# Four-layer graph network on one core: late units in another slot order, residuals moved, wide products a row earlier, last chunk in halves

## The reference

```
x = ln(x + adj @ (scale * (adj @ (x @ W0))) + bias0)
x = ln(x + relu(inv_deg * (a*adj + (1-a)*I) @ x @ W1.T + b1))
d = 1 / sqrt(rowsum(adj))
z = leaky_relu(d * (adj @ (d * x)) @ Wz + bz)
S = exp(-sqrt(dist2(z, z)) / 2), the 4 nearest of each row kept
A2 = S + adj;  d2 = 1 / sqrt(rowsum(A2))
x = ln(x + d2 * (A2 @ (d2 * x)) @ W2 + b2)
x = ln(x + relu(concat(x, adj @ x) @ W3.T + b3))
```

## Time and profile before

| | us |
|---|---|
| median of 3 runs (lowest, highest) | 1446.29 (1445.66, 1446.74) |
| the profiled execution | 1442.02 |
| its span, first to last instruction | 1440.5 |
| TensorE busy | 1389.3 (96%) |
| VectorE busy | 835.8 (58%) |
| ScalarE busy | 445.5 (31%) |
| mean granted clock of TensorE | 0.992 |

### The profile page before, as it was taken

The page is one execution under the profiler, slowest core; times in us unless marked ns, Lnnn a source line. Parts: engine busy times, 40 slices in busy tenths (PEclk is TensorE's granted clock), DMA queues, the critical chain, the costliest instruction groups (busy, mean ns, idle before and its releaser), DMA issues.

```text
span 1440.5 us, 20058 instructions
## 1 busy us (share of the span) xinstructions
PE 1389.3 (96%) x7268; PEld 731.8 (51%) x7268; DVE 835.8 (58%) x1311; ACT 445.5 (31%) x955; POOL 243.7 (17%) x354
## 2 busy tenths in 40 slices
PE   6999999999999999999999999999999979999997
PEld 4776666666544445454544444333333334444454
DVE  5878766666323533433322269999999556655044
ACT  4767665655200000000000047655555200000011
POOL 2111110110100100000000001111111177774000
PEclk9999999999999999999999999999999989999999
DMA  9999998887999969988777614014444889999862
GB/s 301 402 397 389 357 329 310 318 309 258 351 379 360 372 265 395 408 314 336 295 299 299 247 55 136 16 31 133 134 136 136 308 336 371 387 392 397 349 244 65
DMA packets 124850, 407.51 MB, mean 283 GB/s; under 512 B 10624, under 2 KB 40928, under 8 KB 103264
## 3 DMA queue, kind: packets, MB, share of 16 engines
q1 hardware_dynamic: 84704, 315.38, 59.0%
q0 software_dynamic: 20000, 74.97, 13.7%
q10 hardware_dynamic: 20064, 16.04, 3.3%
HBM read 339.77 MB, written 66.58 MB: 282 GB/s over the span
## 4 chain that ended last, share of the span: by engine, by line
PE 66%; DVE 21%; DMA 8%; ACT 2%; POOL 1%; issue 1%; ACTq 0%; DVEq 0%; SPq 0%; POOLq 0%
PE acc L1168 9%; PE acc L1170 9%; PE acc L1169 9%; DVE hT L1053 8%; PE pt L1232 6%; DVE wT L1054 5%; PE pt L1168 4%; PE pt L1170 4%; PE pt L1169 4%; DMA region<-in_adj 4%; DVE wz_sb L1054 3%; PE acc L1213 3%; PE acc L1217 3%; PE acc L1215 3%; PE pxT L1204 1%; PE pxT L1205 1%
## 5 line engine op out<-in xcount | busy, mean ns | idle before, releaser
L1232 PE MATMUL pt<-ident,region 128*128 128x128 f32 x1024 | 243.2, 277 | 19.7 <-DMA region<-in_adj 10.8
L1168 PE MATMUL acc<-region,yop 128*128 128x512 f16 x581 | 220.4, 379 | 5.1 <-DMA region<-at_scratch 5.1
L1169 PE MATMUL acc<-region,yop 128*128 128x512 f16 x581 | 220.2, 379 | 0.0
L1170 PE MATMUL acc<-region,yop 128*128 128x512 f16 x581 | 220.2, 379 | 0.0
L999 DVE SCALAR_TENSOR_TENSOR region<-pt,region 128x512 f16<-128x512 f32 x200 | 135.4, 687 | 75.2 <-ACT region L649 74.9
L1232 PEld LDWEIGHTS pt<-ident,region 128*128 128x128 f32 x1024 | 146.1, 143 | 61.9 <-issue 15.6
L695 ACT ACTIVATE region<-pt 128x512 f32<-128x512 f32 x256 | 132.8, 603 | 114.2 <-PE pt L1328 46.3
L649 ACT ACTIVATE region<-pt 128x512 f16<-128x512 f32 x200 | 117.8, 595 | 106.3 <-PE pt L1232 89.6
L1053 DVE MAX8 hT<-region 128x8 f32<-128x4096 f32 x32 | 141.3, 4414 | 2.9 <-ACT region L695 2.9
L616 ACT ACTIVATE std<-mv,eps_ln 128x4 f32<-128x4 f32 x32 | 9.5, 297 | 343.6 <-DVE mv L833 343.6
L1321 PE MATMUL pt<-yop 128*128 128x512 f16 x256 | 97.4, 380 | 8.1 <-ACT region L695 7.2
(11 more groups left out here) (235 smaller groups left out, 2219.6 us busy)
## 6 DMA issues: line engine op xcount, KB each, us to landing
region<-at_scratch SPq DMA_DIRECT2D x162, 1280.0 KB, 7.7
region<-in_adj SPq DMA_DIRECT2D x64, 1024.0 KB, 9.3
at_scratch<-region POOLq DMA_DIRECT2D x40, 768.0 KB, 7.0
at_scratch<-region POOLq DMA_DIRECT2D x40, 512.0 KB, 7.5
region<-at_scratch SPq DMA_DIRECT2D x76, 256.0 KB, 2.7
region<-at_scratch ACTq DMA_DIRECT2D x4, 1280.0 KB, 8.3
x_scratch<-xout ACTq DMA_DIRECT2D x16, 256.0 KB, 10.8
gath_all<-x_scratch POOLq DMA_DIRECT2D x12, 256.0 KB, 6.6
```

Of the source, the lines that this page charges most:

```text
L1168: nc.tensor.matmul(into, y[:, 0, kt, :], high, start=(kt == first_tile), stop=False)
L1169: nc.tensor.matmul(into, y[:, 0, kt, :], low, start=False, stop=False)
L1170: return nc.tensor.matmul(into, y[:, 1, kt, :], high, start=False, stop=(kt == last_tile))
L1232: ins = nc.tensor.transpose(pt[kt % 4][:, t * P:(t + 1) * P], nat[u % 4][:, t, (kt % TPC) * P:(kt % TPC + 1) * P], ident[:, :])
```

## The change

- Late units: the first four take slots 4, 3, 2, 1, then the order 4, 3, 0, 2, 1 repeats. ScalarE issues three of them instead of four; SyncE issues the fourth after the `y` stores and waits for the wide chunks' end only ahead of the first unit in slot 0.
- Residual rows: the four loads of x2 rows go from SyncE to ScalarE's queue. On VectorE the bias is added before the first mix, and the residuals of chunks 0 to 3 stand together ahead of the second mix tile.
- `WIDE_LAG` is 6 instead of 7; `SUMS_AHEAD` is 5 instead of 4.
- Last pass: ScalarE's copies of the next chunk stand ahead of `act_finish`; chunk 7 is made in two halves of 256 columns, in two banks, each projected, normalized and stored by itself; `finish_chunk` places are closer together.

The core of the diff:

```diff
-LATE_ORDER = [4, 3, 2, 1, 0]
+LATE_FIRST = [4, 3, 2, 1]
+LATE_ORDER = [4, 3, 0, 2, 1]
-WIDE_LAG = 7
+WIDE_LAG = 6
 WIDE_AT = {i: i - WIDE_LAG for i in range(WIDE_LAG, 32)}
-SUMS_AHEAD = 4
+SUMS_AHEAD = 5
-FINISH_AT = {(6, 0): 0, (6, 9): 1, (6, 18): 2, (6, 27): 3, (7, 4): 4, (7, 13): 5, (7, 22): 6}
-RESIDUAL_AT = {(0, 2): [0], (0, 3): [1], (0, 4): [2], (1, 1): [3], **{(c, 3): [c + 3] for c in range(1, 5)}}
+FINISH_AT = {(6, 0): 0, (6, 8): 1, (6, 16): 2, (6, 24): 3}
+FINISH_HALVES_AT = {(0, 0): 4, (0, 16): 5, (1, 0): 6}
+FIRST_HALF_AT = 18
+RESIDUAL_AT = {(0, 1): [0, 1, 2, 3], **{(c, 3): [c + 3] for c in range(1, 5)}}
...
# SyncE
-                if kt == RES_AT:
-                    sp.wait_ge(near_full, KT * NCH)
-                    for t in range(TPC):
-                        sp.dma_start(res_rows(t // 2, 0, NCH)[:, :, t % 2, :], x2_rows[:, t, :, :]).then_inc(res_loaded, 16)
...
-            sp.wait_ge(acc_full, nth(ALL, 4, WIDE - 1))
+            for b in range(2):
+                sp.wait_ge(y_stored[b], 16 * NCH // 2)
             for k in range(ACT_LATE, len(LATE)):
+                if k == LATE_TILES:
+                    sp.wait_ge(acc_full, nth(ALL, 4, WIDE - 1))
                 load_late(sp, k)
...
# ScalarE
                 if i == KT:
+                    act.wait_ge(near_full, KT * NCH)
+                    for t in range(TPC):
+                        act.dma_start(res_rows(t // 2, 0, NCH)[:, :, t % 2, :], x2_rows[:, t, :, :]).then_inc(res_loaded, 16)
                     act.wait_ge(near_used, KT - 1)
                     load_late(act, 0)
...
-            for c in range(NCH):
-                act_epilogue(act, 5, c, None)
+            turned_x3(0)
+            sums5(0)
+            for c in range(NCH - 2):
+                turned_x3(c + 1)
+                sums5(c + 1)
+                act_finish(act, 5, c)
+            turned_x3(NCH - 1)
+            sums_half(0)
+            act_finish(act, 5, NCH - 2)
+            sums_half(1)
...
# VectorE
-                    if (c, t) == (0, 1):
+                    if (c, t) == (0, 0):
                         residual_bias()
...
+            for h in range(2):
+                last_half(h)
...
# TensorE
-            wide_products(25)
+            wide_products(26)
             kept_narrow(NARROW_KEPT[1])
-            wide_products(26)
             wide_products(27)
...
+            for h in range(2):
+                pe.wait_ge(hT_ready, bank_left(NCH - 1) + h)
+                for kt in range(KT):
+                    last = half_columns(h, kt)
+                    if (h, kt) in FINISH_HALVES_AT:
+                        finish_chunk(FINISH_HALVES_AT[h, kt])
+                    if (h, kt) == (1, FIRST_HALF_AT):
+                        project_half(0)
+                last.then_inc(acc_full, 1)
+            project_half(1)
```

More of the change, by code:

```diff
@@ L62 @@
 NARROW_KEPT = [4, 5]
-ACT_LATE = 4
-RES_AT = 26
+ACT_LATE = 3
 A_SCALE = 64.0
@@ L221, in pass_acc, with half_acc @@
             return pt[AHEAD2.index(c)] if p == 2 and c in AHEAD2 else acc[par]
+        def half_acc(h):
+            return wide[1 + h][:, h * HALF:(h + 1) * HALF]
         def late_acc(p, c):
@@ L306, in gnn_kernel @@
                 + [(5, c, u) for c in range(WIDE5, NCH) for u in range(UPC)])
-        LATE_SLOTS = [LATE_ORDER[k % UPC] for k in range(len(LATE))]
+        LATE_SLOTS = LATE_FIRST + [LATE_ORDER[k % UPC] for k in range(len(LATE) - len(LATE_FIRST))]
+        LATE_TILES = LATE_SLOTS.index(0)
         def ends_chunk(k):
@@ L747, in projection_step @@
                     turned_x2(k)
+            x2_rows = x_dram[2].rearrange("(c t p) f -> p t c f", p=P, t=TPC)
             projection_step(0)
@@ L772, in _ @@
                     degrees(g)
-            act.wait_ge(yop_ready, nth(YOP, "y", NCH - 1))
-            for b in range(2):
-                act.wait_ge(y_stored[b], 16 * NCH // 2)
-            load_late(act, ACT_LATE - 1)
             act.wait_ge(xT_ready, nth(XTS, 4, NCH - 1))
@@ L1081, in _ @@
                 close_mix(c)
-            for c in range(NCH):
+            for c in range(NCH - 1):
                 epilogue(5, c, None)
+            for h in range(2):
+                last_half(h)
         def pe_turn(pe, p, c, x3=None, par=None, m=None):
@@ L1482, in finish_chunk, with project_half, half_columns @@
                     pe_turn(pe, 5, c + 1, ((c + 1) % X3_BUFFERS, (c + 1) // X3_BUFFERS + 1))
-            for c in range(WIDE5, NCH):
+            def project_half(h):
+                n = nth(ALL, 5, NCH - 1) + h
+                pe.wait_ge(hT_ready, n)
+                pe.wait_ge(xT_ready, nth(XTS, 5, NCH - 1))
+                pe.wait_ge(nat_read, n - 1)
+                for t in range(TPC)[h * TPC // 2:(h + 1) * TPC // 2]:
+                    nc.tensor.matmul(late_nat[:, t, :], xT[:, t * P:(t + 1) * P], wT[:, 1, :], start=True, stop=False)
+                    last = nc.tensor.matmul(late_nat[:, t, :], hT[:, t * P:(t + 1) * P], wT[:, 2, :], start=False, stop=True)
+                last.then_inc(nat_full, 1)
+            def half_columns(h, kt):
+                c = NCH - 1
+                if kt < KEPT:
+                    hi, lo = (kept[:, c, kt, part, h * HALF:(h + 1) * HALF] for part in range(2))
+                else:
+                    u, within = divmod(kt - KEPT, UNIT)
+                    k = LATE.index((5, c, u))
+                    slot = LATE_SLOTS[k]
+                    if within == 0:
+                        pe.wait_ge(late_loaded_unit[slot], 16 * late_loads(k))
+                    hi, lo = (ring[slot][:, within, part, h * HALF:(h + 1) * HALF] for part in range(2))
+                return products(5, half_acc(h), kt, hi, lo)
+            for c in range(WIDE5, NCH - 1):
                 for kt in range(KT):
@@ L1491, in _ @@
                 last.then_inc(acc_full, 1)
-            pe_project(pe, 5, NCH - 1)
+            for h in range(2):
+                pe.wait_ge(hT_ready, bank_left(NCH - 1) + h)
[7 more added lines that the diff above has]
+            project_half(1)
 LATE_PARAMS = 3
```

48 lines of the change are left out of this document (46 added, 2 removed).

## The result

The changed kernel takes 1470.88 us (median of 4, 1468.16 to 1474.10); beside it the kernel before took 1445.97 (median of 4, 1440.01 to 1446.74). The ratio is 1.0185, 95% interval 1.0162 to 1.0207: slower, clear of the noise; whether by 2% the interval leaves open. 1472.5 was predicted, in a range of 1453 to 1483. The profiled execution took 1469.73 us with a span of 1468.2; the mean granted clock fell from 0.992 to 0.985.

What follows compares the result with a forecast made beforehand. VectorE was taken to bound the search, TensorE close behind; later products and loads are level. 37.3 (search) - 7.3 (gate) - 3.8 (end) = 26.2 us longer than 1442.02: 1468.2, plus 4.3 to the median, 1472.5; range 1453 to 1483.

Steps and rivals of the forecast that it cites:

- The bound: In the neighbour search VectorE sets the pace, TensorE close behind with only 1.2 us free in four rows.
- the lag's step: Neighbour search: at a lag of six TensorE waits for GpSimd's low part; 22.6 us plus 14.7 for the clock, 37.3 longer.
- the seven rows named: Search rows 6, 10, 14, 18, 22, 26 and 30, where TensorE was to wait for the operand.
- The first wait: First operand wait in the search: VectorE loses 2.2 us, plus 2.1 for the clock; later ones 3.4 each plus clock.
- The clock's term: Search, behind each operand wait: TensorE runs at half speed, 2.1 us at each of seven places, 14.7 us.
- Rival C: Neighbour search not slowed, operand ready or VectorE having a finished row in hand; faster, 1435.2 us; chance 0.07.
- B: Neighbour search: the clock holds or recovers at once after the waits; 9.4 us longer, 1455.7 us; chance 0.20.
- The gate's step: Sixth pass, k-tiles 12 to 16 needing VectorE's chunk 4: TensorE and gate come earlier, a gain of 7.3 us.
- the term that failed: Gathers ahead of the sixth pass's gate: with the bias moved, two long gathers go and the gate comes 3.0 us earlier.
- the 1.9 us kept for the range: GpSimd's plain store of `y` beside the moved bias might be held 0 to 1.9 us; taken as 0.
- The end: Last pass: 1.8 us from copies ahead of `finish`, 2.0 from the last chunk in halves, 3.8 us gained (3.1 to 4.5).
- The halves: Last chunk made in two halves of 256 columns: net gain 2.0 us at the kernel's end.

Runs made afterwards that it cites:

- wait_filled: Changed kernel with 15 never-read products of 512 columns ahead of the operand wait in rows 6, 10, ... 30; 1457.08 us, ratio 1.0076.
- wait_half_filled: wait_filled with 8 products instead of 15; 1468.14 us, ratio 1.0163.
- before_gate: Kernel before with the 18 products of kept k-tile 2 ahead of the gate at k-tile 12 of pass 5; 1444.72 us, ratio 1.0007.
- end_alone: Kernel before with the change's last part only: copies ahead of act_finish, closer finish places, last chunk in halves; 1439.10 us, ratio 0.9940.
- bias_back: lag6_half_row with the residual bias back behind the first mix tile; 1440.07 us, ratio 0.9959.
- lag7_rest: Changed kernel with WIDE_LAG back at 7 and the products of k-tile 25 back behind the search; 1438.21 us, ratio 0.9955.
- lag7_res_back: lag7_rest with the residuals of chunks 0 to 3 back between the mix tiles, the bias staying ahead; 1436.33 us, ratio 0.9936.
- lag6_half_row: Changed kernel with each wide product half a row later, so the operand wait stands behind the row's second banks; 1432.76 us, ratio 0.9923.
- res_back: lag6_half_row with the residuals of chunks 0 to 3 back between the mix tiles, the bias staying ahead; 1437.04 us, ratio 0.9950.
- gate_filled: lag6_half_row with the 18 products of kept k-tile 2 ahead of the gate at k-tile 12 of pass 5; 1426.63 us, ratio 0.9866.
- whole_last: lag6_half_row with the last chunk whole again (512 columns, one projection, one store); 1436.74 us, ratio 0.9935.

## Why the prediction was right, point by point

**The bound and the lag's step: right.** Waits of 4.74 and 4.65 us stood for 4.6 predicted, in the seven rows named, in front of the product named and released by GpSimd's low part. The wait's price of 3.4 us per four rows was 3.56 (wait_filled), that of the clock 1.65 instead of 2.1, since the slow stretch behind a wait of 4.74 us was 2.6 us long (901.96 to 904.6) and behind one of 4.65 us 3.4 (1024.2 to 1027.6), not the 3 to 5.6 of the earlier trace rows. The first wait, priced at 2.2 + 2.1, cost VectorE 3.94 us of idle time. The clock's term was thus the one mis-sized in this step, by 0.45 us at each of seven places. Together 36.7 less the 1.5 that stood there earlier is 35.2 where 37.3 was predicted. Rival C (the search isn't slowed) and B (the clock holds) are out by the trace; wait_filled is B made real in the search, at 1457.1 us where B was priced at 1455.7.

By the rule cited from the Trainium skill (TensorE: Matmul & The Clock Gate, HAM oscillation), a loop with a pause in each round starts every round at the low clock: the seven waits of 4.74 and 4.65 us agree. The pauses in the page's case last some 3 to 5 us. Of the seven shorter ones in wait_half_filled, of 1.94 and 2.01 us, the clock fell behind five.

**The gate's step: 4.2 us instead of 7.3.** TensorE reached the gate 11.7 us earlier against the search's end (9.2 predicted), waited there, and its clock fell (nine products at half speed, 1.9 us, where 2.1 was taken). The 9.2 were made up otherwise than predicted: TensorE's idle time between search and gate fell from 11.0 to 3.3 us, by 7.7 where two waits of together 5.0 had been counted, the 3.9 us of lost clock went too, and of the 2.6 us for twelve products, which the prediction named but left out of its sum, the lost lead took 2.1 (together 12.1 of such terms, for the 11.7). And the prediction's own figures didn't fit each other: with TensorE 9.2 and the gate 9.4 us earlier no wait is left, so nothing for a fall of the clock. The wait of 5.6 us came of the earlier arrival (2.5) and above all of the term that failed, the 3.0 us by which the gate itself was to come earlier: it came 0.3 later (130.5 instead of 130.2). The gathers did come earlier, the 80th at 101.0 us behind the first instead of 103.7, no one over 1.4 us. But the first came 0.3 later, the mix tile that takes the last of chunk 4 stood 6.67 us behind the 80th gather's issue instead of 4.91 (1295.67 - 1289.00 and 1259.60 - 1254.69), and VectorE waited 0.86 us for its own store of the chunk before. The page has that store (`x_scratch<-xout`) at 16.6 us from issue to landing, before at 10.8. So in these two traces the transfers behind the gathers took back what GpSimd had won; before, the DMA share is 1.00 from 1250 us on the earlier trace rows. Which transfer held the last gather up was not tried, and part may be scatter: before_gate and end_alone, whose mix is that of the kernel before, have the gate at 133.3 and 130.7. In bias_back the bias, put back, moves the gate by 4.3 us, so in the changed order it matters; that moving it gained anything from before to after, where the gate stands at 130.2 and 130.5, no run shows.

The rule on two SBUF inputs (the Trainium skill, SBUF — State Buffer, Who interferes with whom) agrees with the gathers: two of 2.96 and 2.02 us beside the bias in bias_back, none over 1.4 us in the changed kernel. The plain store of `y` beside the bias in its new place took 0.82 us (at 1180.50), as in the kernel before (0.82 at 1143.78), so the 1.9 us kept for the range were not needed.

**The end: 4.9 us instead of 3.8.** The halves brought 2.3 (2.0 predicted), the copies ahead of `act_finish` and the closer finish places 2.5 to 2.6 instead of 1.8. Two projections begin 1418.47 - 1411.07 = 7.40 us apart; 24 products of eight k-tiles are 5.18 of them, so turning and projecting take 2.22 us. Before it was 1396.43 - 1387.93 = 8.50 us, less 27 products (5.82) 2.68. So a place gives 0.46 us where 0.3 was taken, though the trace of before has the wait of 0.18 us at five of the seven places only, not at six.

**The sum: a cancellation helped.** 26.2 us were predicted between two profiled executions, 27.7 came: 2.1 less at the search, 1.5 from before it, 3.1 less gain behind it, 1.1 more at the end. Between the medians it is 24.9, since the profiled execution of before was 4 us under its median and that of the changed kernel 1.2; the 4.3 us added for that were 3.1 too many, the sum was 1.5 too small, and the prediction came out 1.6 too high. That it lies so near is luck in part.

**Not seen in the prediction.** What the change is worth without the wait: 0.5 to 0.6% at a lag of seven (lag7_rest, lag7_res_back), 0.8% with the half-row shift. That the parts of the change are tied, since four residuals in a row need a TensorE that is early for its projections, is suggested by lag7_rest and not shown.

## What to carry to other kernels

Before work is moved a step ahead, find in the trace when its operand is ready and what stands in order behind it: asked for between the two groups of banks the operand cost 5.2 us in four rows, asked for half a row later it cost nothing. A pause of TensorE has two prices, the work that isn't done and the slow products behind it; other work in the pause can save the second even if it can't save the first (15 products did, 8 mostly did not). And a wait that appears at a gate after a gain is the next thing to fill: 18 products that were ready anyway were worth 6 us there.

## What the runs showed of the hardware that I had not expected

Equal waits of TensorE can end in different clocks. In wait_half_filled the waits in rows 10 and 14, both of 2.01 us behind eight products and the same rows of work, were followed by 0.38 and by 0.62 us products. At the first tile wait behind the search, slow products follow waits of 2.00 us (lag6_half_row, nine of them) and 2.13 (res_back), and none follow 2.09 (bias_back), 2.10 (gate_filled) and 2.20 (whole_last). The wait of 1.73 us in the last search row is followed by slow products in lag7_rest and by none in the kernel before and lag7_res_back. No row shows what decides.
